# A software-pipelined windowed-attention stack: the rotary halves are exchanged by accumulating DMAs, dense matmul runs are issued in two halves, and a norm, a copy and the squares of a LayerNorm change place

## The chip, the cores and the metric

The kernel runs on one core of a Trainium2 chip. Its time is the device time of one execution in microseconds. Six engines appear in the profile: PE (TensorE; its weight loads are shown apart as PEld), DVE (VectorE), ACT (ScalarE), POOL (GpSimd), SP (SyncE, which here only issues DMAs) and the DMA engines. Each compute engine runs its own instruction stream; the streams meet in semaphores.

## What is computed

The program computes two blocks with conditioned LayerNorms. The middle of it, and most of its time, is a stack of six layers of windowed attention and a gated feed-forward network, on a batch of 4, 1024 tokens each, width 128:

```python
for i in range(DEPTH):                                   # DEPTH = 6
    x = attn_layer(shift_tokens(x), Wqkv[i], q_scale[i], k_scale[i], Wo[i]) + x
    x = ffn_layer(shift_tokens(x), ln_g[i], ln_b[i], W1[i], b1[i], W2[i], b2[i]) + x

def attn_layer(x, Wqkv, qs, ksc, Wo):                    # 16 heads of 64
    q, k, v = (sh(t) for t in jnp.split(x @ Wqkv, 3, -1))
    q, k = l2norm(q) * qs, l2norm(k) * ksc
    q = q * cos * scale + rotate_half(q) * sin * scale   # rotary embedding
    k = k * cos * inv + rotate_half(k) * sin * inv
    out = local_attention(q, k, v)                       # windows of 32, each sees itself and the one before
    return out.transpose(0, 2, 1, 3).reshape(b, n, INNER) @ Wo
```

`ffn_layer` is a LayerNorm, a matmul to twice 341 channels, `a * gelu(gate)` and a matmul back. Everything is float32. Ahead of the stack stand one attention over all tokens (`theta_attention`) and a LayerNorm; behind it stand a scan over tokens and a mixture of experts (`recurrence_and_mixture`).

## The kernel before

`local_layers` first normalizes x in eight chunks of 512 tokens (`LayerNorm`: mean on PE, `centred` on DVE, squares on ACT, variance on PE, a Newton square root on DVE, a spread on PE, `normed` on DVE, output on ACT; each waits for the one before). Then 96 units of work, 16 blocks of 256 tokens times 6 layers, go through a software pipeline. `pipelined(eng, step)` runs one hand-written order, `step(at)`, on each engine, once per unit: `at(k)` is the unit that entered k steps ago, so one step works on six units at once: projections of q and k of `at(1)` and `at(2)`, scores, softmax and weighted values of `at(3)`, output projection of `at(4)`, feed-forward of `at(5)` and `at(6)`. Six steps fill the pipeline, a hardware loop of 45 iterations runs two steps each (an even and an odd one, because many buffers are doubled), six steps drain it.

What an engine does next is set by the written order alone. A PSUM area is written again only when its last reader is done (`vacated(...)` waits on those semaphores). There are three pairs of PSUM banks (`pairs[0]` to `pairs[2]`) and two single ones.

On PE the dense runs are `scores(x)` (two mask matmuls, L957, then 64 float32 matmuls, which the trace counts as 128, L964) and `weighted(x)` (the same number, L1001), each with its own weight load, x being the half of the unit's tokens. Around them stand `project` (L920), `values` (L977), `norms` (L930), `hidden` (L1054), `out_projection` (L1021), `spread` (L947), `probs_across` (L986), `outputs_across` (L1011) and the LayerNorm of the feed-forward part (L1029 mean, L1036 variance, L1044 spread).

The rotary embedding works on four parts i of 128 x 1024 values (i = 0, 1 keys, 2, 3 queries). DVE multiplies the projection by the cosine table into `mcos` (`rotate_cos`, L1272) and by the sine table into `msin` (`rotate_sin`, L1281); SP copies `msin` with even and odd partitions exchanged into `swapped` by two DMAs (`halves_across`, L756); POOL adds `mcos` and `swapped` into `ks` or `qr` (`rotated`, L873):

```python
dst = (ks if i < 2 else qr[u.odd])[:, 4 * g:4 * g + 4, :].rearrange("p g t -> p (g t)")
nc.gpsimd.tensor_tensor(dst, mcos[i % 2][:, :], swapped[:, :], ALU.add).then_inc(rope_add, 1)
```

Then `scale_keys` (L1320) multiplies `ks` by its inverse norms into `kr`, and `scores` reads `kr` and `qr`. Of the softmax, DVE takes row maxima (`maxima`, L1330, and the tiny L1332, `ebias`), ACT the exponentials (L1172), PE transposes (L986), ACT copies (`probsT`). `outputs` (L1348) scales the attention result into `o`; `gated` (L1393) writes `act_out`.

Of the kernel before, what the change touches and what calls it, by code (L numbers as in the profile page):

```python
# [137 lines left out]
class LayerNorm:  # L138


# [17 lines left out]
    def tensor_mean(self, pe, n, src, wide):  # L158
        nc, c = self.nc, self.const

        pe.wait_ge(self.normed_ready, START + n)
        nc.tensor.matmul(wide, c["mean_w"][:, :], src, start=True, stop=True).then_inc(self.mean_ready, 1)  # L162
# [35 lines left out]
    def vector_normed(self, dve, n, wide, gain):  # L198
        nc = self.nc
        dve.wait_ge(self.spread_ready, START + n + 1)  # L200
        dve.wait_ge(self.out_ready, START + n)
# [439 lines left out]
def local_layers(nc, const, t):  # L641

    ctx = ExitStack()
    with ctx:
# [43 lines left out]
        ln = LayerNorm(nc, ctx, "loc_ln", const, sem, (sq[:, 0, 0:CH], sq[:, 0, CH:], sq[:, 1, 0:CH]))  # L688
# [5 lines left out]
        hs_ready, qk_ps, sq_ready, rot, rope_add = sem("hs_ready"), sem("qk_ps"), sem("sq_ready"), sem("rot"), sem("rope_add")  # L694
        swap_ready = [sem(f"swap_ready{i}") for i in range(4)]
# [18 lines left out]

        def pipelined(eng, step):
# [4 lines left out]
            for s in range(FILL):  # L720
                step(filling(s))
            with nc.Fori(FILL // 2, TOTAL // 2, engines=bass.OrderedEngineSet([eng.engine]), hint_back_edge=True) as i:
                for odd in range(2):
                    step(lambda k: Unit(2 * i + (odd - k), (odd - k) % 2))
            for s in range(TOTAL, TOTAL + FILL):
                step(filling(s))

        @block.sync
        def _(sp):
# [16 lines left out]

            def halves_across(i, u):

                if u is None:
                    return  # L750
                after(sp, rot, u.n, 8, 2 * i + 2)
                own_wait(sp, passed)
                after(sp, rope_add, u.n, 4, i)
                own_wait(sp, passed)
                for half in range(2):
                    sp.dma_start(swapped[1 - half:P:2, :], msin[half:P:2, :]).then_inc(swap_ready[i], 16)  # L756
# [24 lines left out]
            def step(at, refill=lambda name: None):  # L781
                halves_across(1, at(2))
                refill("wk")
                halves_across(2, at(2))
                even_windows(0, at(3))
                halves_across(3, at(2))
                refill("wq")
                halves_across(0, at(1))
# [52 lines left out]
        def _(pool):  # L841
# [20 lines left out]
            def rotated(i, u):  # L862
# [1227 lines left out]
```

## Time and profile before

| | |
|---|---|
| median of 3 runs (lowest, highest) | 4979.43 us (4970.4, 4989.21) |
| the profiled execution | 4985.01 us, span 4983.1 us |
| mean granted clock of TensorE | 0.950 |
| busy share: PE, DVE, ACT, POOL | 81%, 74%, 63%, 22% |
| mean share of the 16 DMA engines of its largest queue | 20.4% |

The times of the groups below are microseconds from the start of the span. A busy share is a mean over all stages; a wait in brackets stands in front of the instruction that waited, with what released it. "issue" is a wait that ended with nothing that the profile shows.

### The profile page before, as it was taken

The numbers are of one execution on the slowest core, as the hardware profiler recorded it, in microseconds if no ns is written. First come the engines' busy times: TensorE is split into PE (matmuls) and PEld (weight loads), VectorE is DVE, ScalarE is ACT, GpSimd is POOL, SyncE is SP. The second block draws the span as 40 slices with busy tenths as digits, with TensorE's granted clock in tenths as the row PEclk, the third lists the DMA queues.
The fourth block names the chain that finished last, engine by engine and source line by source line (L and its number), as shares of the span: only waits on it lengthen the run. The fifth ranks groups of instructions, "written<-read, shape, count | busy, mean of one in ns | idle before, by whom it ended". The sixth has DMA issues, their size and how long they took to land. (4 is left out here: it accounts for less than half of the span.)

```text
span 4983.1 us, 174228 instructions
## 1 busy us (share of the span) xinstructions
PE 4053.0 (81%) x68188; PEld 2876.0 (58%) x68188; DVE 3701.7 (74%) x6683; ACT 3147.4 (63%) x8447; POOL 1095.9 (22%) x856
## 2 busy tenths in 40 slices
PE   7947888888888888888888888888888888886578
PEld 4725566665666666665666656666666666654234
DVE  4837777777777877777777777787777777774765
ACT  4715766666666666766666667667766667663233
POOL 0002222222222222222222222222222222220112
PEclk9959999999999999999999999999999999997688
DMA  0012222222222222222222222222222222220000
GB/s 26 1 58 82 72 76 73 75 91 78 70 77 71 82 85 78 76 74 74 88 82 77 74 76 80 87 78 78 74 74 90 83 78 73 75 75 24 0 7 11
DMA packets 126167, 336.76 MB, mean 68 GB/s; under 512 B 32592, under 2 KB 33744, under 8 KB 125264
## 3 DMA queue, kind: packets, MB, share of 16 engines
q1 hardware_dynamic: 125520, 326.63, 20.4%
q8 instruction: 590, 9.67, 0.9%
q14 instruction: 57, 0.47, 0.0%
HBM read 22.41 MB, written 2.10 MB: 5 GB/s over the span
## 5 line engine op out<-in xcount | busy, mean ns | idle before, releaser
L1172 ACT ACTIVATE loc_probs<-loc_pair,loc_ebias,loc_rnorm 128x64 f32<-128x64 f32 x3072 | 1200.6, 433 | 10.9 <-DVE loc_ebias L1332 7.8
L873 POOL TENSOR_TENSOR loc_ks<-loc_mcos,loc_swapped 128x1024 f32<-128x1024 f32 x192 | 452.1, 2354 | 1776.6 <-DVE loc_kr L1320 1375.0
L920 PE MATMUL loc_pair<-loc_hs,loc_wqk 128*128 128x256 f32 x3072 | 751.4, 388 | 47.5 <-issue 43.1
L873 POOL TENSOR_TENSOR loc_qr<-loc_mcos,loc_swapped 128x1024 f32<-128x1024 f32 x192 | 452.2, 2355 | 1270.6 <-DMA loc_swapped<-loc_msin 1204.6
L1172 ACT ACTIVATION_READ_ACCUMULATOR loc_probs<-loc_pair,loc_ebias,loc_rnorm 128x1 f32 x3072 | 719.6, 234 | 0.0
L920 PEld LDWEIGHTS loc_pair<-loc_hs,loc_wqk 128*128 128x128 f32 x3072 | 568.0, 192 | 151.9 <-issue 64.4
L1330 DVE TENSOR_REDUCE loc_mx<-loc_pair 128x8 f32<-128x512 f32 x384 | 264.5, 689 | 410.1 <-PE loc_pair L964 402.9
L1272 DVE SCALAR_TENSOR_TENSOR loc_mcos<-loc_pair,loc_scal,loc_tab 128x1024 f32<-128x1024 f32 x384 | 490.5, 1277 | 86.7 <-ACT loc_sq L1154 65.3
L1154 ACT ACTIVATE loc_sq<-loc_pair 128x1024 f32<-128x1024 f32 x384 | 396.9, 1034 | 204.2 <-PE loc_pair L920 204.2
L1281 DVE SCALAR_TENSOR_TENSOR loc_msin<-loc_pair,loc_scal,loc_tab 128x1024 f32<-128x1024 f32 x384 | 489.6, 1275 | 9.1 <-DMA loc_swapped<-loc_msin 8.9
L964 PE MATMUL loc_pair<-loc_kr,loc_qr 64*32 64x64 f32 x24576 | 322.9, 226 | 122.0 <-issue 121.4
L1183 ACT ACTIVATE loc_vodd<-loc_pair 128x1024 f32<-128x1024 f32 x192 | 196.9, 1025 | 349.2 <-DMA loc_veven<-loc_vodd 210.5
L977 PE MATMUL loc_pair<-loc_wv,loc_hs 128*64 128x512 f32 x1536 | 408.3, 656 | 1.6 <-DVE loc_o L1348 1.4
L964 PEld LDWEIGHTS loc_pair<-loc_kr,loc_qr 64*32 64x32 f32 x24576 | 273.9, 106 | 221.6 <-issue 219.2
L1332 DVE SCALAR_TENSOR_TENSOR loc_ebias<-loc_mx,loc_rnorm 128x8 f32<-128x8 f32 x384 | 379.8, 989 | 13.2
L1001 PE MATMUL loc_pair<-loc_veven,loc_probsT 64*32 64x64 f32 x12288 | 307.7, 226 | 86.2 <-issue 83.9
L1197 ACT ACTIVATE loc_oT<-loc_pair 128x1024 f32<-128x1024 f32 x192 | 195.0, 1016 | 271.0 <-PE loc_pair L1011 271.0
L1190 ACT ACTIVATE loc_probsT<-loc_pair 128x1024 f32<-128x1024 f32 x192 | 195.8, 1020 | 268.8 <-PE loc_pair L986 268.8
L1021 PE MATMUL loc_one<-loc_oT,loc_wo 128*128 128x256 f32 x1536 | 347.5, 379 | 0.8 <-DVE loc_act_out L1393 0.4
L1001 PEld LDWEIGHTS loc_pair<-loc_veven,loc_probsT 64*32 64x32 f32 x12288 | 261.5, 105 | 149.6 <-issue 148.7
L1054 PE MATMUL loc_one<-loc_h,loc_w 128*128 128x256 f32 (+1 forms) x1152 | 322.1, 403 | 17.1 <-DVE loc_act_out L1393 7.3
L1001 PE MATMUL loc_pair<-loc_vodd,loc_probsT 64*32 64x64 f32 x12288 | 314.9, 226 | 3.7 <-issue 3.7
(228 smaller groups left out, 7457.6 us busy)
## 6 DMA issues: line engine op xcount, KB each, us to landing
loc_swapped<-loc_msin SPq DMA_DIRECT2D x768, 256.0 KB, 2.6
loc_veven<-loc_vodd SPq DMA_DIRECT2D x768, 64.0 KB, 2.2
loc_veven<-loc_vodd SPq DMA_DIRECT2D x384, 128.0 KB, 2.3
loc_wqk<-wqk_dram SPq DMA_DIRECT2D x12, 512.0 KB, 4.6
loc_wv<-wv_dram SPq DMA_DIRECT2D x6, 512.0 KB, 4.1
loc_wo<-wo_dram SPq DMA_DIRECT2D x6, 512.0 KB, 4.5
x<-xT_dram SPq DMA_DIRECT2D x1, 2048.0 KB, 7.4
loc_tab<-tables_dram SPq DMA_DIRECT2D x1, 2048.0 KB, 7.6
```

Source lines behind the costliest of these rows:

```text
L873: nc.gpsimd.tensor_tensor(dst, mcos[i % 2][:, :], swapped[:, :], ALU.add).then_inc(rope_add, 1)
L920: ins = nc.tensor.matmul(pairs[b][:, p // 2, (p % 2) * UNIT:(p % 2 + 1) * UNIT], wqk[:, k, w:w + P], hs[u.odd][:, :], start=True, stop=True)
L964: ins = nc.tensor.matmul(pairs[b][WIN * w:WIN * w + WIN, hp, p * 2 * WIN:(p + 1) * 2 * WIN], qr[u.odd][part, p, at:at + WIN], kr[u.odd][pa ...
L977: ins = nc.tensor.matmul(pairs[b][hp * DH:(hp + 1) * DH, g, :], hs[u.odd][:, BLK * x + DH * g:BLK * x + DH * g + DH], wv[:, hp, :], start= ...
L1001: ins = nc.tensor.matmul(pairs[b][WIN * w:WIN * w + WIN, hp, p * DH:(p + 1) * DH], probsT[part, p, WIN * w:WIN * w + WIN], v[part, w // 2, ...
L1021: ins = nc.tensor.matmul(bank(b)[:, 0:UNIT], wo[:, p, :], oT[:, p, :], start=p == 0, stop=p == PAIRS - 1)
L1054: ins = nc.tensor.matmul(bank(b)[0:FB[j], k * UNIT:(k + 1) * UNIT], w1[:, at:at + FB[j]], h[:, :], start=True, stop=True)
L1154: nc.scalar.activation(sq[:, i, :], flat(b), ACT.Square).then_inc(sq_ready, 1)
L1172: ins = nc.scalar.activation(probs[x][:, p, hp, :], pairs[b][:, hp, p * 2 * WIN:(p + 1) * 2 * WIN], ACT.Exp, bias=ebias[x][:, k:k + 1], sc ...
L1272: nc.vector.scalar_tensor_tensor(mcos[i % 2][:, :].rearrange("p (g t) -> p g t", g=4), flat(b).rearrange("p (g t) -> p g t", g=4), scal[u. ...
L1281: nc.vector.scalar_tensor_tensor(msin[:, :].rearrange("p (g t) -> p g t", g=4), flat(b).rearrange("p (g t) -> p g t", g=4), scal[u.odd][:, ...
L1332: nc.vector.scalar_tensor_tensor(ebias[x][:, k], mx[x][:, k], -1.0, rnorm[u.odd][:, x, HEADS:].rearrange("p (g y) -> p y g", y=2)[:, hp, : ...
```

## The change

1. Rotary: `rotate_cos` writes straight into `ks` or `qr` (`ks` is now doubled), `rotate_sin` writes into `msin[i % 2]`, and POOL issues two DMAs per part that add the exchanged halves into place. SP's copies, POOL's additions, `mcos`, `swapped` and the semaphore `rope_add` are gone; `landed` waits for the DMAs.
2. PE: in even steps `scores(1)`, `weighted(0)` and `scores(0)` are issued in two halves with other matmuls between, and the head of PE's loop is put at a fixed place, `head_slot` 208.
3. `ln_squares` moves from the start of ACT's step to DVE, behind `centre`.
4. On DVE `widen(0)` (the copy of the inverse norms, L1309) moves ahead of `rotate_cos(0)`.
5. The LayerNorm ahead of the stack takes chunks in pairs, with two sets of buffers, and the wait for the constants with two casts stands behind it.

```diff
-        mcos = [sb(f"mcos{i}", [P, HALF_Q]) for i in range(2)]
-        msin, swapped = sb("msin", [P, HALF_Q]), sb("swapped", [P, HALF_Q])
-        qr, ks = [sb(f"qr{i}", [P, PAIRS, UNIT]) for i in range(2)], sb("ks", [P, PAIRS, UNIT])
+        msin = [sb(f"msin{i}", [P, HALF_Q]) for i in range(2)]
+        qr, ks = ([sb(f"{s}{i}", [P, PAIRS, UNIT]) for i in range(2)] for s in ("qr", "ks"))
...
-                for half in range(2):
-                    sp.dma_start(swapped[1 - half:P:2, :], msin[half:P:2, :]).then_inc(swap_ready[i], 16)
...
+                after(pool, rot, u.n, 8, 2 * i + 2)
                 own_wait(pool, passed)
-                g = i % 2
-                dst = (ks if i < 2 else qr[u.odd])[:, 4 * g:4 * g + 4, :].rearrange("p g t -> p (g t)")
-                nc.gpsimd.tensor_tensor(dst, mcos[i % 2][:, :], swapped[:, :], ALU.add).then_inc(rope_add, 1)
+                for half in range(2):
+                    there = rotated_part(i, u)[1 - half:P:2, :, :].rearrange("p g t -> p (g t)")
+                    pool.dma_start(there, msin[i % 2][half:P:2, :], accum_op=ALU.add).then_inc(swap_ready[i], 16)
...
+            with nc.Fori(FILL // 2, TOTAL // 2, engines=bass.OrderedEngineSet([eng.engine]), hint_back_edge=True,
+                         head_slot={eng.engine: 208} if eng is nc.tensor else None) as i:
...
-                    scores(1, at(3), 2)
+                    scores(1, at(3), 2, whole if odd else (0,))
...
+                if not odd:
+                    scores(1, at(3), 2, (1,))
...
-                    weighted(0, at(3), 1)
+                    weighted(0, at(3), 1, whole if odd else (0,))
...
+                if not odd:
+                    weighted(0, at(3), 1, (1,))
                 if at(2) is not None:
                     vacated(pe, ((o_ready, at(3), 4, 2), (rot, at(1), 8, 2),))
-                    scores(0, at(2), 1)
+                    scores(0, at(2), 1, whole if odd else (0,))
...
+                if not odd:
+                    scores(0, at(2), 1, (1,))
                 ln_mean(at(4), 4)
...
-                after(dve, swap_ready[i - 1], u.n - (i == 0), SWAP, SWAP)
+                landed(dve, i - 2, u.n - (i < 2))
...
             def step(at, odd):
                 maxima(0, 1, at(3), 1)
                 centre(at(5), 4)
+                ln_squares(at(5))
...
+                widen(0, at(2))
                 rotate_cos(0, at(1), 1)
-                widen(0, at(2))
...
                 for c in range(2):
-                    ln.vector(dve, b * 2 + c, x[:, bass.ds(b * SEQ + c * CH, CH)], bank(0), bank(1)[:, 0:4], mods[:, 1:2])
+                    lns[c].vector_centre(dve, b * 2 + c, x[:, bass.ds(b * SEQ + c * CH, CH)], bank(c))
+                for c in range(2):
+                    lns[c].vector_rstd(dve, b * 2 + c, bank(2 + c)[:, 0:4])
+                for c in range(2):
+                    lns[c].vector_normed(dve, b * 2 + c, bank(c), mods[:, 1:2], b * 2)
```

The order of PE in the even step of the loop, around `scores(1)`, before (L957 mask, L964 scores, L920 `project(3)`, L977 `values(1)`, L930 `norms`; the counts are of instructions in the code, and the trace shows each float32 matmul as two, x128 for x64):

```order
L957 MATMUL loc_pair<-loc_mask,loc_ident 128x512 x2
L964 MATMUL loc_pair<-loc_kr,loc_qr 32x64 x64
L920 MATMUL loc_pair<-loc_hs,loc_wqk 128x256 x4
L977 MATMUL loc_pair<-loc_wv,loc_hs 64x512 x4
L134 ISA
L127 ISA
L930 MATMUL loc_one<-loc_sq,loc_head_sum 32x256 x16
```

The same place of the change (L961, L968, L919, L982 and L929 are the same calls):

```order
L961 MATMUL loc_pair<-loc_mask,loc_ident 128x512 x2
L968 MATMUL loc_pair<-loc_kr,loc_qr 32x64 x32
L919 MATMUL loc_pair<-loc_hs,loc_wqk 128x256 x4
L968 MATMUL loc_pair<-loc_kr,loc_qr 32x64 x32
L982 MATMUL loc_pair<-loc_wv,loc_hs 64x512 x4
L134 ISA
L127 ISA
L929 MATMUL loc_one<-loc_sq,loc_head_sum 32x256 x16
```

The second half of the scores now stands behind `project(3)`.

The end of PE's even step before, behind `weighted(0)` (L1054 `hidden(2)`, L986 `probs_across(1)`, L1011 `outputs_across(0)`, L947 `spread(1)`, L1029 `ln_mean`):

```order
L1001 MATMUL loc_pair<-loc_vodd,loc_probsT 32x64 x2
L134 REGISTER_ALU
L1054 MATMUL loc_one<-loc_h,loc_w 85x256 x2
L986 MATMUL loc_pair<-ident,loc_probs 128x128 x8
L957 ISA
L957 MATMUL loc_pair<-loc_mask,loc_ident 128x512 x2
L964 MATMUL loc_pair<-loc_kr,loc_qr 32x64 x64
L1011 MATMUL loc_pair<-ident,loc_o 128x128 x8
L134 REGISTER_ALU
L947 MATMUL loc_pair<-ident,loc_rk_wide 128x128 x8
L1029 MATMUL loc_one<-loc_xb,mean_w 128x256
```

The same place of the change, from the last row of `weighted(0)` (L1007) on; its first half stands ahead of `hidden(2)` (L1061):

```order
L1007 MATMUL loc_pair<-loc_vodd,loc_probsT 32x64 x2
L725 ISA
L961 ISA
L961 MATMUL loc_pair<-loc_mask,loc_ident 128x512 x2
L968 MATMUL loc_pair<-loc_kr,loc_qr 32x64 x32
L1018 MATMUL loc_pair<-ident,loc_o 128x128 x8
L134 REGISTER_ALU
L946 MATMUL loc_pair<-ident,loc_rk_wide 128x128 x8
L968 MATMUL loc_pair<-loc_kr,loc_qr 32x64 x32
L1036 MATMUL loc_one<-loc_xb,mean_w 128x256
```

Now nothing stands between the last matmul of `weighted(0)` and the mask of `scores(0)`, and the scores end behind `spread(1)`.

## Rows read from the trace of the kernel before

**Rows 1.** Busy time by stretch: the six filling steps, the loop

```profile
core 0: us, PE busy (x) PEld busy (x) DVE busy (x) ACT busy (x) POOL busy (x), PEclk, DMA share, GB/s
...
345.00:498.00 153.00, 115.08 (x2077) 83.60 (x2078) 106.08 (x160) 78.41 (x239) 42.13 (x30) 0.90 0.24 81
498.00:4417.00 3919.00, 3289.26 (x61935) 2394.85 (x61934) 3055.70 (x5315) 2689.48 (x7564) 956.20 (x721) 0.98 0.25 78
```

**Rows 2.** Who PE waited for, 500 to 4400: total us, times, longest

```profile
PE loc_one L930 <- DVE loc_act_out L1393: 134.0, 81, 2.3
PE loc_pair L964 <- issue: 117.9, 90, 2.2
PE loc_pair L1001 <- issue: 81.3, 88, 1.5
PE loc_pair L947 <- ACT loc_probs L1172: 76.4, 86, 0.9
PE loc_one L1036 <- ACT loc_lsq L1204: 61.5, 50, 1.4
PE loc_one L1044 <- DVE loc_rstd L95: 52.4, 41, 1.8
PE loc_one L1063 <- issue: 46.4, 44, 1.6
PE loc_pair L920 <- issue: 29.5, 43, 1.1
```

**Rows 3.** Timeline of PE, one even step: start, us, instruction, idle before

```profile
2273.07 1.94 PE L977 MATMUL loc_pair<-loc_wv,loc_hs 128*64 128x512 f32 x8
...
2291.22 0.25 PE L1001 MATMUL loc_pair<-loc_veven,loc_probsT 64*32 64x64 f32 x2 [1.23 <-issue]
...
2291.50 1.09 PE L1054 MATMUL loc_one<-loc_h,loc_w 128*85 128x256 f32 x4
2292.43 1.04 PE L986 MATMUL loc_pair<-ident,loc_probs 128*128 128x128 f32 x8
2293.30 0.59 PE L957 MATMUL loc_pair<-loc_mask,loc_ident 128*128 x2
2293.83 1.28 PE L964 MATMUL loc_pair<-loc_kr,loc_qr 64*32 64x64 f32 x95
2297.04 0.46 PE L964 MATMUL loc_pair<-loc_kr,loc_qr 64*32 64x64 f32 x33 [1.93 <-issue]
```

**Rows 4.** The page's DMA queues, the one that brings instructions: packets, MB, share

```profile
q8 instruction: 590, 9.67, 0.9%
```

**Rows 5.** The page's costliest groups: DVE's smallest operation

```profile
L1332 DVE SCALAR_TENSOR_TENSOR loc_ebias<-loc_mx,loc_rnorm 128x8 f32<-128x8 f32 x384 | 379.8, 989 | 13.2
```

**Rows 6.** Timeline of DVE, the same iteration

```profile
2256.18 1.91 DVE L1332 SCALAR_TENSOR_TENSOR loc_ebias<-loc_mx,loc_rnorm 128x8 f32<-128x8 f32 x1
...
2277.57 1.27 DVE L1281 SCALAR_TENSOR_TENSOR loc_msin<-loc_pair,loc_scal,loc_tab 128x1024 f32<-128x1024 f32 x1
...
2291.66 1.29 DVE L1348 TENSOR_TENSOR loc_o<-loc_pair,loc_recip 128x512 f32<-128x512 f32 x2 [0.70 <-PE loc_pair L1001]
...
2298.51 0.17 DVE L1332 SCALAR_TENSOR_TENSOR loc_ebias<-loc_mx,loc_rnorm 128x8 f32<-128x8 f32 x1
```

**Rows 7.** Timeline of POOL, the same iteration

```profile
2255.73 2.35 POOL L873 TENSOR_TENSOR loc_ks<-loc_mcos,loc_swapped 128x1024 f32<-128x1024 f32 x1 [14.18 <-DVE loc_kr L1320]
```

**Rows 8.** The page's DMA issues: KB each, median us from issue to landing

```profile
loc_swapped<-loc_msin SPq DMA_DIRECT2D x768, 256.0 KB, 2.6
```

**Rows 9.** Timeline of all engines ahead of the stack and in its LayerNorm

```profile
253.86 0.34 SPq L733 DMA_DIRECT2D loc_tab<-tables_dram  x1
...
262.67 0.43 DVE L1248 CAST loc_mask<-loc_sq 128x512 bf16<-128x512 f32 x1 [13.82 <-DMA loc_params<-params_dram]
...
283.34 2.07 PE L162 MATMUL loc_pair<-x,mean_w 128*128 x2 [0.93 <-DVE loc_sq L202]
...
293.32 2.07 PE L162 MATMUL loc_pair<-x,mean_w 128*128 x2 [0.93 <-DVE loc_sq L202]
```

More of the change, by code:

```diff
@@ L713, in local_layers, with rotated_part, landed @@
         LAST_USE = {"wk": 1, "wq": 1, "wv": 2, "wo": 3, "w1": 4, "w2": 5}
+        def rotated_part(i, u):
+            g = 4 * (i % 2)
+            return (ks if i < 2 else qr)[u.odd][:, g:g + 4, :]
+        def landed(eng, i, n):
+            if not isinstance(n, int) or n >= 0:
+                eng.wait_ge(swap_ready[i], SWAP * n + SWAP)
         def pipelined(eng, step):
@@ L720, in pipelined @@
             for s in range(FILL):
-                step(filling(s))
-            with nc.Fori(FILL // 2, TOTAL // 2, engines=bass.OrderedEngineSet([eng.engine]), hint_back_edge=True) as i:
+                step(filling(s), s % 2)
+            with nc.Fori(FILL // 2, TOTAL // 2, engines=bass.OrderedEngineSet([eng.engine]), hint_back_edge=True,
+                         head_slot={eng.engine: 208} if eng is nc.tensor else None) as i:
                 for odd in range(2):
-                    step(lambda k: Unit(2 * i + (odd - k), (odd - k) % 2))
+                    step(lambda k: Unit(2 * i + (odd - k), (odd - k) % 2), odd)
             for s in range(TOTAL, TOTAL + FILL):
-                step(filling(s))
+                step(filling(s), s % 2)
         @block.sync
@@ L1064, in ffn_out, with step @@
                 ins.then_inc(y_ps, 1)
-            def step(at):
+            whole = (0, 1)
+            def step(at, odd):
                 if at(2) is not None:
@@ L1197, in outputs_out @@
                 nc.scalar.activation(oT[:, :, BLK * x:BLK * x + BLK], flat(b).rearrange("p (g t) -> p g t", g=PAIRS), ACT.Copy).then_inc(oT_ready, 1)
-            def ln_squares(u):
-                if u is None:
-                    return
-                after(act, xc_ready, u.n)
-                after(act, var_ps, u.n - 1)
-                nc.scalar.activation(lsq[:, :], xc[:, :], ACT.Square).then_inc(lsq_ready, 1)
             def h_out(u):
@@ L1219, in gelus, with step @@
                                      bias=fpar[u.odd][0:FB[j], 3 + NFB + j:4 + NFB + j]).then_inc(gelu_ready, 1)
-            def step(at):
-                ln_squares(at(5))
+            def step(at, odd):
                 square(2, at(2), 2)
@@ L1315, in scale_keys @@
                 after(dve, spread_ps, u.n, 2, x + 1)
-                after(dve, rope_add, u.n, 4, 2)
+                for i in range(2):
+                    landed(dve, i, u.n)
                 after(dve, sim_ps, u.n - 2, 2, 2)
@@ L1405, in residual_ffn, with step @@
                 ins.then_inc(xa_done, 1)
-            def step(at):
+            def step(at, odd):
                 maxima(0, 1, at(3), 1)
                 centre(at(5), 4)
+                ln_squares(at(5))
                 gated(2, at(6), 3)
```

127 lines of the change are left out of this document (67 added, 60 removed).

## The prediction

> **What bounds the kernel now.** I read the stretches first [rows 1]: the loop runs from 498 to 4417, 45 iterations in 3919 us, so 87.1 us for two steps, and the six filling steps take 153 us, the draining ones about as long. PE is busy for 3289.26 / 45 = 73.1 us of an iteration, DVE for 67.9, ACT for 59.8; the granted clock is 0.98, so TensorE stands at its upper level all through the loop and the clock has nothing to give. No engine is full. What ends an iteration is PE's chain, and it is idle for 14.0 of 87.1 us. The second view is whom PE waited for [rows 2]; divided by the 3900 / 87.1 = 44.8 iterations of its window, the idle time is
>
> - issue (nothing that the profile shows): (117.9 + 81.3 + 46.4 + 29.5) / 44.8 = 6.1 us
> - `act_out` from DVE ahead of `norms`: 3.0 us
> - `probs` from ACT ahead of `spread`: 1.7 us
> - `lsq` from ACT: 1.4 us; `rstd` from DVE: 1.2 us
>
> That is 13.4 of the 14.0 us. The change goes at each of these but the third.
>
> What the issue waits are: in the timeline of PE [rows 3] one ends at 2291.22 inside `weighted(0)` and the next at 2297.04 inside `scores(0)`. Between them stand 16 matmuls (eight rows of two, of which the first is shown) + 4 + 8 + 2 + 95 = 125, each with a weight load, 250 instructions and a few register and semaphore instructions. The queue that brings instructions moved 9.67 MB in 590 packets, 16.4 KB each [rows 4]. Both fit one reading: PE's code comes in blocks of about 256 instructions, and a block that is used up faster than the next one arrives leaves PE waiting. A dense run (128 matmuls with 128 loads) uses a whole block in some 1.5 us (1.28 us for 95 of 128 matmuls [rows 3]), every other piece of the step takes several times that for as many instructions. In the even half dense runs and block ends meet, in the odd half they don't; the counts in [rows 2], 43 to 90, are one or two for an iteration.
>
> What makes DVE late: `ebias`, 128 x 8 values, takes 0.17 us alone and 1.91 us at 2256.18, where it ends with POOL's addition of 2255.73 + 2.35 = 2258.08 [rows 6, 7]. Its mean over 384 is 0.989 us [rows 5], 0.82 us too much; there are 384 / 96 = 4 in a step and 8 in an iteration, so this smallest operation alone loses 6.6 us of DVE's 67.9: DVE stands still while POOL adds. The small steps of the two Newton roots stand in the same place.
>
> The Trainium skill (SBUF — State Buffer, section Who interferes with whom) says that a DVE instruction with two SBUF inputs contends with a GpSimd instruction that reads SBUF, and that the later one is fully blocked. By that, the trace agrees: `ebias` reads two SBUF tiles, and 1.91 against 0.17 us is the block. The same page has a rule that speaks against this change: a DMA of GpSimd's queue needs descriptors that GpSimd writes itself, and VectorE's copies in two-port modes starve it. No row here shows it; its price is taken up under the third rival.
>
> **The change part by part.** Per iteration of the loop, against 87.1 us.
>
> *Rotary.* Removed: POOL's eight additions of 2.35 us and SP's sixteen issues. DVE's own multiplications stay as they are (1.27 us [rows 6]), with another destination. Added: sixteen DMA issues on POOL. POOL is busy for 956.20 / 45 = 21.2 us of 87.1 [rows 1], of which 8 x 2.35 = 18.8 us goes away, so even at 4 us an issue it has room. DVE is no longer blocked. I credit only what PE waits for: of the 3.0 us ahead of `norms` the half that the blocks make (see below for the other half), **-1.6 us**; of `rstd` all, -1.2 us. From below this part could give nothing, if DVE is blocked by the issues as it is by the additions; from above 4.2.
>
> What must land in time: queries of part 3. `rotate_sin(3)` ends at 2277.57 + 1.27 = 2278.84 [rows 6], and the mask of `scores(0)` starts at 2293.30 [rows 3], 14.5 us later. Today an exchange takes 2.6 us from issue to landing [rows 8], the addition 2.35 more. No row shows a DMA that adds, so its cost lies between those 2.6 us and anything; I take twice a plain one for each of the pair, some 10 us together, and it is hidden by `norms` to `probs_across(1)`. The keys have longer still. The work behind it on POOL, the copy of the next tokens, waits for two issues more; `project(0)` needs it, but two halves later.
>
> *Splits and the loop's place.* The order shows PE's even step cut after 32 of 64 matmuls, with 1.9 to 2 us of `project(3)` behind the first half, and so on. Kept are the issue waits ahead of the split runs: at `project(2)` 29.5 / 43 = 0.7, at the first `weighted(1)` 0.6 (the mean of its 88 waits is 0.92, the second of each pair 1.23 [rows 2, 3]) and in the feed-forward's last matmuls 46.4 / 44 = 1.05: 2.3 us. Gone or shrunk: 1.2 in `weighted(0)` and 117.9 / 44.8 = 2.6 in the two `scores`, 3.8 us; I leave 0.3 us of them: **-3.5 us**. From below: if half a run is still too dense, half of it, -1.9.
>
> The splits also add waits. The second half of `weighted(0)` now stands straight ahead of the mask of `scores(0)`, which waits for `outputs(0)`, the reader of that pair, two operations in 1.29 us [rows 6]. Before, `hidden(2)` and `probs_across(1)` stood between, 2293.30 - 2291.50 = 1.8 us [rows 3]. With the hops of the semaphores **+1.3 us**. And `scores(1)` ends 2 us later, while DVE's row maxima, `ebias`, the residual and `gated(0)` still stand ahead of `act_out`: about 3.7 us of work, with only `values(1)`, 1.94 us [rows 3], to cover it. So of `norms`' wait, 1.4 us stays in the even half; that is the other half of the 3.0 above.
>
> *Squares to DVE, the copy ahead.* DVE squares 256 columns in about 0.4 us and PE need not wait for ACT's queue: **-1.4 us** (`lsq`), and with `rstd` above **-2.5 us** in all. DVE has room: 67.9 less at least 6.6 of blocks. `widen(0)` first: ahead of `spread(0)`, which waits for ACT's `probs` and not for the copy, so nothing.
>
> *Handed on.* The wait on ACT's `probs`, 0.9 us in each half, stays: ACT's row of two times eight exponentials and a table load is no shorter. Once PE is early at `outputs_across(1)` in the odd half, it meets the `probs` of `exponentials(0, 1)` there. Between 0 and all of the 2.5 us saved ahead of it; ACT is only 59.8 / 81 busy, so it is latency, not load, and I take **+0.5 us**.
>
> *LayerNorm ahead.* A chunk takes 293.32 - 283.34 = 10.0 us [rows 9], nearly all of it one engine waiting for another. In a pair the second chunk runs in the gaps of the first; I take 15 us a pair, so -5 us times four pairs, -20 (bounds 0 and -40). It also begins without the constants: DVE stood for 13.8 us until 262.67, SP began to load at 253.86 [rows 9]: another -8. **-28 us** in all.
>
> **Sum.** -1.6 - 2.5 - 3.5 + 1.3 + 0.5 = -5.8 us an iteration, 81.3 instead of 87.1, times 45 = -261 us. Filling and draining have the same waits in emptier steps (PE busy 115 of 153 us while filling): -15. With -28: -304. Against the profiled execution, 4985.01, this gives 4681; it lay 5.6 us above the median, so 4675 us.
>
> **The rivals.**
>
> *First, the same mechanisms with other sizes.* If the halves of runs still wait for code, or ACT takes back all that DVE gives (+2 instead of +0.5), an iteration saves 3 us: 135 + 15 + 28, so about 4800. If both new waits are covered and the code waits at the head fall too, it saves 8: about 4580. For the first speaks that four things must hold at once; for the second, that the next limit is PE's own 73.1 us.
>
> *Second, the additions land late (the other side, slower).* Each microsecond by which part 3 lands after the mask of `scores(0)` is ready costs a microsecond in each of the 96 steps. The gain is 304 / 96 = 3.2 us a step, so the change loses when from the end of `rotate_sin(3)` to landing more than 14.5 + 3.2 = 17.7 us pass. At 20 us it is 5.5 x 96 - 304 = +224: 5200 us. For it speaks that two DMAs of 256 KB that read, add and write are issued by POOL, behind other issues, by a way that no row shows; against it that 17.7 us is nearly seven times the 2.6 us of a plain one [rows 8], and that the DMA engines are busy for 25% [rows 1].
>
> *Third, DVE is blocked all the same.* POOL's descriptor work may hold DVE as its additions do, or DVE's copies may hold POOL. Then the 1.6 and 1.2 us are not saved, the late scores add 1.4 us ahead of `norms`, and the square, now in front of the root, is blocked too, as are operations that sixteen issues meet where eight additions did not; for these I take 1.6 us, two blocks as in [rows 6]. -3.5 - 1.4 + 1.3 + 0.5 + 1.4 + 1.6 = -0.1 us an iteration; with the LayerNorm's -28 it is about 4945, no change that can be told from none with certainty.
>
> By the skill's starvation rule, named above, `widen`'s float32 copies would hold up POOL's issues where DVE and POOL meet; what that does to the time is the second rival's price, and no row shows such a meeting.
>
> **How the numbers follow.** Main case, 4590 to 4750: 0.60. Smaller gain, 4750 to 4870: 0.17. Larger gain, 4500 to 4590: 0.08. DVE still blocked, 4920 to 5000: 0.05. Late landing, over 5005: 0.10. The predicted time is the main one's, 4675. From 4560 to 4850 lies 0.8 of it: the main case, most of the smaller gain and a part of the larger. Runs of before spread by 0.4%, so about 0.5% is what a measurement can tell from no change: below 4954 is faster, 0.86; same 0.04; slower 0.10.
>
> **What would show it.** Right: `ebias` at 0.17 us throughout and DVE's busy time in the loop down by 6 us an iteration or more; no waits for `lsq` and `rstd`; issue waits of about 2.5 us an iteration, none in the `scores` and the second `weighted`; a new wait for `o` of over 1 us ahead of the mask; `act_out` at 1.4 us in even halves alone; an iteration of 80 to 83 us. Wrong: a wait of PE for the accumulating DMAs ahead of L961, `ebias` still near 1 us, issue waits that only moved to the other halves, or a wait on ACT's `probs` of over 3 us an iteration.

## The result and the profile after

The changed kernel takes 4730.99 us (median of 4 runs, 4725.08 to 4750.15), the kernel before 4978.07 us: a ratio of 0.9509, interval 0.9476 to 0.9541. 247 us were saved; 304 had been forecast (4675 us), and 4731 us lies inside the range of 4560 to 4850. The profiled execution has a span of 4723.2 us, 259.9 less than before.

First the stretches of the changed kernel; the columns are those of [rows 1]. They are the LayerNorm ahead of the stack, the filling steps, the loop, the draining steps and the tail.

```profile
249.00:303.00 54.00, 33.86 (x113) 19.97 (x114) 27.85 (x118) 16.52 (x24) 1.85 (x9) 0.61 0.25 95
303.00:450.00 147.00, 117.34 (x2085) 84.82 (x2084) 91.78 (x164) 79.91 (x239) 36.30 (x50) 0.91 0.44 86
450.00:4161.00 3711.00, 3287.78 (x61924) 2385.57 (x61925) 2541.97 (x5402) 2658.90 (x7471) 741.14 (x1080) 0.98 0.41 82
4161.00:4308.00 147.00, 116.68 (x2040) 83.85 (x2039) 75.61 (x194) 86.03 (x251) 12.84 (x20) 0.92 0.23 47
4308.00:4723.30 415.30, 282.42 (x865) 141.39 (x864) 261.84 (x571) 120.58 (x165) 74.62 (x75) 0.76 0.02 8
```

Against [rows 1] the loop is 3711 us long instead of 3919, so an iteration is 82.5 us instead of 87.1: 208 us. It begins at 450 instead of 498. Of these 48 us the filling steps give 6 (147 instead of 153) and the LayerNorm with its start 42. The remaining 4 us lie behind the loop. PE's busy time in the loop is what it was (3287.78 against 3289.26 us), so all the gain of the loop is idle time of PE. DVE's busy time has fallen from 67.9 to 56.5 us an iteration.

Whom PE waits for in the changed kernel, 480 to 4200, 45.1 iterations (compare [rows 2]; L961 is the mask, L929 `norms`, L946 `spread`, L1007 `weighted`, L982 `values`, L919 `project`, L1061 `hidden`, L1043 the variance):

```profile
PE loc_pair L961 <- DVE loc_o L1363: 116.8, 90, 2.0
PE loc_one L929 <- DVE loc_act_out L1415: 96.2, 50, 2.2
PE loc_pair L946 <- ACT loc_probs L1187: 61.8, 71, 0.9
PE loc_pair L1007 <- issue: 53.2, 47, 1.6
PE loc_pair L982 <- issue: 18.5, 44, 0.8
PE loc_pair L919 <- issue: 16.5, 38, 2.8
PE loc_one L1061 <- DVE loc_act_out L1415: 16.2, 46, 0.4
PE loc_one L1043 <- DVE loc_lsq L1391: 11.1, 44, 0.3
PE loc_pair L1007 <- DVE loc_kr L1335: 10.2, 45, 0.2
...
PE loc_one L929 <- issue: 7.3, 25, 0.3
```

An iteration has 2.1 us of issue waits (6.1 before) and none of note in the scores. `rstd` is gone from the list and `lsq` is 0.25 us (2.5 before for both). But `o` has risen from 0.2 to 2.6 us, and `act_out` is still 2.1 us ahead of `norms`, where 1.4 had been forecast, and 0.4 us more ahead of `hidden`.

The even step of the changed kernel in PE's timeline, 2290 to 2315, shows what the splits brought:

```profile
2292.98 1.93 PE L929 MATMUL loc_one<-loc_sq,loc_head_sum 128*32 128x256 f32 x32 [2.17 <-DVE loc_act_out L1415]
...
2306.24 1.10 PE L1061 MATMUL loc_one<-loc_h,loc_w 128*85 128x256 f32 x4 [0.35 <-DVE loc_act_out L1415]
2307.37 1.09 PE L991 MATMUL loc_pair<-ident,loc_probs 128*128 128x128 f32 x8
...
2311.19 0.60 PE L961 MATMUL loc_pair<-loc_mask,loc_ident 128*128 x2 [1.94 <-DVE loc_o L1363]
2311.72 1.11 PE L968 MATMUL loc_pair<-loc_kr,loc_qr 64*32 64x64 f32 x64
2312.76 1.97 PE L1018 MATMUL loc_pair<-ident,loc_o 128*128 128x128 f32 x8
```

The mask stands behind the second half of `weighted(0)` and waits 1.94 us for `outputs(0)`. What follows is slower as well: `outputs_across` lasts 1.97 us, against 1.09 us for the eight matmuls of the same shape in `probs_across` (L991). The granted clock of the stretches around the waits, with the columns of [rows 1], shows why:

```profile
2293.00:2297.00 4.00, 4.00 (x43) 2.85 (x44) 2.93 (x7) 2.39 (x5) 1.19 (x2) 1.00 0.34 81
...
2300.00:2306.00 6.00, 4.97 (x87) 3.94 (x85) 3.68 (x6) 5.97 (x20) 1.92 (x3) 1.00 0.60 149
...
2311.00:2315.00 4.00, 3.81 (x77) 3.23 (x78) 2.56 (x3) 0.23 (x1) 1.46 (x2) 0.60 0.04 7
2315.00:2320.00 5.00, 4.77 (x154) 3.94 (x155) 3.03 (x6) 4.25 (x13) 0.73 (x2) 0.98 0.54 102
```

The granted clock is 1.00 ahead of the wait of 1.94 us and 0.60 for the 4 us behind it, mostly the lower of its two levels (1.2 of 2.4 GHz), then 0.98. By these rows this wait costs up to 4 x 0.4 = 1.6 us more (an estimate). Not every wait does: behind the 2.17 us ahead of `norms`, 18 us earlier, the clock stays at 1.00 (first row). What tells the two apart is not shown by any run here.

In DVE's timeline, the same place:

```profile
2309.29 1.29 DVE L1363 TENSOR_TENSOR loc_o<-loc_pair,loc_recip 128x512 f32<-128x512 f32 x2 [1.97 <-PE loc_pair L1007]
...
2317.62 0.17 DVE L1347 SCALAR_TENSOR_TENSOR loc_ebias<-loc_mx,loc_rnorm 128x8 f32<-128x8 f32 x1
```

`ebias` takes 0.17 us again. Below are its group in the changed kernel and, from its page, the cost and landing of the accumulating DMAs:

```profile
L1347 DVE SCALAR_TENSOR_TENSOR loc_ebias<-loc_mx,loc_rnorm 128x8 f32<-128x8 f32 x384 | 85.7, 223 | 13.2
...
L868 POOL DMA_DIRECT2D loc_qr<-loc_msin x384 | 332.1, 1006 | 1150.8 <-DVE loc_msin L1295 1133.1
...
loc_ks<-loc_msin POOLq DMA_DIRECT2D x384, 256.0 KB, 4.4
loc_qr<-loc_msin POOLq DMA_DIRECT2D x384, 256.0 KB, 5.0
```

The mean of `ebias` is 223 ns, not 168, its median: POOL still has one small addition that reads SBUF, on the keys (`loc_kr`, L878, 0.60 us). One of them starts at 2319.53, and the `ebias` of 2319.78 takes 0.39 us.

An issue holds POOL for 1.0 us, the landing comes 5.0 us after it (median; 7.7 at the longest): some 6 to 7 us for a pair, where I had taken 10, and far inside the 14.5 us of room.

The LayerNorm ahead of the stack, PE's mean matmuls of two successive pairs of chunks:

```profile
262.75 3.78 PE L163 MATMUL loc_pair<-x,mean_w 128*128 x4 [0.93 <-DVE loc_sq L203]
...
274.83 3.78 PE L163 MATMUL loc_pair<-x,mean_w 128*128 x4 [0.93 <-DVE loc_sq L203]
```

12.1 us a pair, where one chunk took 10.0 [rows 9].

### The profile page after: what moved, and what is told of

Read it like the earlier page. It is cut to its first block and busy times, and to the rows that moved or that the text cites. A ratio compares the mean times of both kernels' runs of the same rounds, so it can differ in the third digit from the quotient of the medians.

```text
span 4723.2 us, 172910 instructions
## 1 busy us (share of the span) xinstructions
PE 4045.2 (86%) x68188; PEld 2863.9 (61%) x68188; DVE 3161.6 (67%) x6779; ACT 3116.9 (66%) x8351; POOL 867.3 (18%) x1240
## 2 busy tenths in 40 slices
DMA packets 126144, 336.58 MB, mean 71 GB/s; under 512 B 32592, under 2 KB 33744, under 8 KB 125264
## 5 line engine op out<-in xcount | busy, mean ns | idle before, releaser
L919 PE MATMUL loc_pair<-loc_hs,loc_wqk 128*128 128x256 f32 x3072 | 745.8, 386 | 25.5 <-issue 17.3
L1187 ACT ACTIVATION_READ_ACCUMULATOR loc_probs<-loc_pair,loc_ebias,loc_rnorm 128x1 f32 x3072 | 709.7, 231 | 0.0
L919 PEld LDWEIGHTS loc_pair<-loc_hs,loc_wqk 128*128 128x128 f32 x3072 | 568.8, 191 | 122.0 <-issue 40.5
L868 POOL DMA_DIRECT2D loc_ks<-loc_msin x384 | 331.5, 1008 | 1278.7 <-DVE loc_msin L1295 1242.0
L868 POOL DMA_DIRECT2D loc_qr<-loc_msin x384 | 332.1, 1006 | 1150.8 <-DVE loc_msin L1295 1133.1
L982 PE MATMUL loc_pair<-loc_wv,loc_hs 128*64 128x512 f32 x1536 | 373.2, 606 | 21.7 <-issue 19.3
L1363 DVE TENSOR_TENSOR loc_o<-loc_pair,loc_recip 128x512 f32<-128x512 f32 x384 | 246.5, 683 | 212.3 <-PE loc_pair L1007 212.1
L1061 PE MATMUL loc_one<-loc_h,loc_w 128*128 128x256 f32 (+1 forms) x1152 | 338.6, 419 | 25.6 <-DVE loc_act_out L1415 24.1
L1007 PE MATMUL loc_pair<-loc_vodd,loc_probsT 64*32 64x64 f32 x12288 | 304.2, 226 | 55.2 <-issue 55.1
L968 PEld LDWEIGHTS loc_pair<-loc_kr,loc_qr 64*32 64x32 f32 x24576 | 268.7, 106 | 111.8 <-issue 111.7
L968 PE MATMUL loc_pair<-loc_kr,loc_qr 64*32 64x64 f32 x24576 | 317.1, 228 | 4.3 <-issue 4.2
L1028 PEld LDWEIGHTS loc_one<-loc_oT,loc_wo 128*128 128x128 f32 x1536 | 291.6, 190 | 41.4 <-DVE loc_act_out L1415 1.2
L1007 PE MATMUL loc_pair<-loc_veven,loc_probsT 64*32 64x64 f32 x12288 | 299.9, 226 | 12.8 <-DVE loc_kr L1335 11.2
L1286 DVE SCALAR_TENSOR_TENSOR loc_ks<-loc_pair,loc_scal,loc_tab 128x1024 f32<-128x1024 f32 x192 | 245.8, 1280 | 85.6 <-ACT loc_sq L1169 84.6
```

The lines of the kernel that those rows point to most:

```text
L868: pool.dma_start(there, msin[i % 2][half:P:2, :], accum_op=ALU.add).then_inc(swap_ready[i], 16)
L919: ins = nc.tensor.matmul(pairs[b][:, p // 2, (p % 2) * UNIT:(p % 2 + 1) * UNIT], wqk[:, k, w:w + P], hs[u.odd][:, :], start=True, stop=True)
L968: ins = nc.tensor.matmul(pairs[b][WIN * w:WIN * w + WIN, hp, p * 2 * WIN:(p + 1) * 2 * WIN], qr[u.odd][part, p, at:at + WIN], kr[u.odd][pa ...
L982: ins = nc.tensor.matmul(pairs[b][hp * DH:(hp + 1) * DH, g, :], hs[u.odd][:, BLK * x + DH * g:BLK * x + DH * g + DH], wv[:, hp, :], start= ...
L1007: ins = nc.tensor.matmul(pairs[b][WIN * w:WIN * w + WIN, hp, p * DH:(p + 1) * DH], probsT[part, p, WIN * w:WIN * w + WIN], v[part, w // 2, ...
L1028: ins = nc.tensor.matmul(bank(b)[:, 0:UNIT], wo[:, p, :], oT[:, p, :], start=p == 0, stop=p == PAIRS - 1)
```

## The experiments

The runs were made in three batches (e1 to e4, e5 to e8, e9 to e12; the last on another chip than the first two). Each has the ratio to the kernel before in its own batch, where that took 4980, 5001 and 4985 us, so ratios are compared, not times. The changed kernel itself was not run again beside the later batches; differences from its 0.9509 of some 0.5% are therefore not told from none.

**The splits undone, and the place undone.** The first run makes the three dense runs whole in even steps, with the loop head at its place:

```diff
-                    scores(1, at(3), 2, whole if odd else (0,))
+                    scores(1, at(3), 2)
...
-                if not odd:
-                    scores(1, at(3), 2, (1,))
```

and so for `weighted(0)` and `scores(0)`.

> The changed kernel with scores(1), weighted(0) and scores(0) whole again in even steps; PE's loop stays at its fixed place. Theory (the splits trade instruction waits for data waits): an iteration of the loop regains about 3.8 us of issue waits inside the scores and the second weighted, and loses the waits that the splits brought, o ahead of the mask (1.9 down to 0.3) and act_out ahead of norms (2.1 down to 0.5), so it is 82.5 + 0.6 = about 83.1 us, the kernel about 4760 us. Rival (the splits alone are what pays): data waits stay, an iteration is 86 us and the kernel about 4890 us.

4700.09 us, ratio 0.946 (0.9434 to 0.9486): not the 4760 us of the theory but, if anything, half a per cent faster than with the splits (the intervals just overlap). The traces' spans are 4698.1 and 4723.2 us, iterations 82.1 and 82.5 us. Whom PE waits for in it, 500 to 4100, 43.9 iterations (L968 scores, L1018 `outputs_across`):

```profile
PE loc_pair L1007 <- issue: 136.4, 89, 3.6
PE loc_pair L968 <- issue: 106.7, 86, 2.7
PE loc_pair L946 <- ACT loc_probs L1181: 79.7, 88, 1.0
PE loc_pair L1018 <- ACT loc_probs L1181: 32.2, 41, 0.9
PE loc_pair L961 <- DVE loc_o L1357: 28.8, 44, 0.7
```

The issue waits are back, 6.7 us an iteration instead of 2.1, and `o` is down to 0.65 and `act_out` to 0.2. The exchange itself is there: 4.6 us of code waits against 4.3 us of waits for DVE. The theory had the first term at 3.8, and it left out PE's own time: in the stretch 500 to 4000 PE is busy for 71.7 us an iteration (3057.80 of 3500) with whole runs and for 73.1 (3101.70 of 3500) with the splits, at a granted clock of 0.99 and 0.98. The splits' waits are followed by slower work more often, and that takes back what they win.

The second run takes away the place alone:

```diff
-            with nc.Fori(FILL // 2, TOTAL // 2, engines=bass.OrderedEngineSet([eng.engine]), hint_back_edge=True,
-                         head_slot={eng.engine: 208} if eng is nc.tensor else None) as i:
+            with nc.Fori(FILL // 2, TOTAL // 2, engines=bass.OrderedEngineSet([eng.engine]), hint_back_edge=True) as i:
```

> The changed kernel without the fixed place of PE's loop head; all else stays. Theory (instruction blocks of 256; where their ends fall decides): the loop's issue waits differ from 2.1 us an iteration, by up to 2 us either way, and they move to other lines. Rival (the splits alone make the waits small, the place means nothing): the same time within 10 us, 4731 us, with waits at the same lines.

4957.97 us, ratio 0.9968 (0.9951 to 0.9984). Without this one number nearly the whole change is lost: 227 us by the medians. I had expected up to 2 us an iteration; it was 5.2, and one line has most of it (L918 is `project(2)`, the first of an iteration; window 500 to 4100, 41 iterations):

```profile
PE loc_pair L918 <- issue: 192.6, 41, 5.2
PE loc_pair L960 <- DVE loc_o L1362: 106.3, 82, 2.0
```

4.7 us, once an iteration, at the loop's head. Its timeline there, the last matmul of one iteration, the first of the next, and the same `project(2)` run in the following step:

```profile
2285.51 0.86 PE L1035 MATMUL loc_one<-loc_xb,mean_w 128*128 128x256 f32 x2
2290.94 3.40 PE L918 MATMUL loc_pair<-loc_hs,loc_wqk 128*128 128x256 f32 x8 [4.57 <-issue]
...
2337.18 1.89 PE L918 MATMUL loc_pair<-loc_hs,loc_wqk 128*128 128x256 f32 x8
```

Behind the wait of 4.57 us the same eight matmuls take 3.40 instead of 1.89 us: the granted clock is 0.58 from 2290.9 to 2295 (1.00 until 2286), and 0.95 over this loop against 0.98.

**Why the place matters.** The page's row of the instruction queue has the number. First the changed kernel, then the one without the place:

```profile
q8 instruction: 591, 9.68, 0.9%
```

```profile
q8 instruction: 633, 10.37, 0.9%
```

42 packets more for 45 iterations: nearly one more an iteration. The loop has 2854 traced instructions of PE an iteration (2846 before). Between issue waits lie 256, and the first lies at the 48th with place 208, so 208 + 2854 = 3062 end within twelve blocks of 256 (3072). Without the place the waits lie some 13 instructions earlier, so the head is at about 221, and 221 + 2854 = 3075 reaches into a thirteenth. The kernel before, 2846 instructions long, has 590 packets [rows 4]: it did not spill. To test it I put the head 16 instructions later, and 32 earlier:

```diff
-                         head_slot={eng.engine: 208} if eng is nc.tensor else None) as i:
+                         head_slot={eng.engine: 224} if eng is nc.tensor else None) as i:
```

> The changed kernel with the loop head 16 instructions later, at place 224. Theory (the loop's 2854 traced instructions on TensorE fit twelve blocks of 256 from place 208, 208 + 2854 = 3062 of 3072; from 224 they spill into a thirteenth, 3078, which is fetched just as the loop jumps back): an issue wait of 4 to 5 us at the first project of each iteration, 45 x 4.7 = 210 us more, the kernel about 4950 us. Rival (the distance of dense runs to block ends is what counts, and 16 instructions shift it little): 4731 us within 30 us.

> The changed kernel with the loop head 32 instructions earlier, at place 176; it fits twelve blocks too. Theory (only the spill matters much): the same time, 4731 us within 40 us, with the issue waits at other instructions. Rival (208 is a sharp best place): over 4800 us.

Place 224: 4988.39 us, ratio 0.9978 (0.9958 to 0.9997), 633 packets, an iteration of 88.7 us, and the wait at the head:

```profile
PE loc_pair L919 <- issue: 180.8, 40, 4.9
```

4.5 us an iteration, as foretold. Place 176: 4801.22 us, ratio 0.960 (0.9565 to 0.9635), 590 packets, 84.3 us an iteration and no such wait. So the spill is worth 0.9978 - 0.960 = 3.8% between two places of one batch, and 0.9978 - 0.9509 = 4.7% against place 208. The exact place among those that fit makes 0.960 - 0.9509 = 0.9%, about 45 us: a little more than the theory's margin of 40, and short of the rival's 4800 us once the batch's slower kernel before is allowed for. With place 176 the issue waits are (64.6 + 39.8 + 11.5) / 41.5 = 2.8 us instead of 2.1, and PE is busy for 74.2 us an iteration instead of 73.1.

**The rotary part alone**, on the kernel before, with the head left to itself and at place 208. The edit is parts 2 to 5 of the change taken back, in the second with the place of part 2 kept.

> The kernel before with the rotary part of the change alone (accumulating DMAs from GpSimd, no additions on it). Theory (GpSimd's additions block VectorE, which is late at act_out and rstd): ebias falls from a mean of 0.99 to 0.17 us, VectorE's busy time by 10 us an iteration, an iteration from 87.1 to about 83.5 us, the kernel about 4810 us. Rival (the exchange only leaves the path of SyncE, or nothing of it is on the path): 4950 to 4980 us.

> The kernel before with the rotary part alone, and PE's loop head at place 208. Theory (without the place this edit lost at the loop head what it gained elsewhere): the wait of 4.3 us at the first project goes, an iteration is 86.8 - 4 = about 82.8 us and the kernel about 4770 us. Rival (the wait at the head is the rotary part's own, for instance from the queue of DMAs): about 4940 us as without the place.

4941.98 us, ratio 0.9928 (0.9897 to 0.9959), and 4802.96 us, ratio 0.9613 (0.9582 to 0.9645). The first time is nearly the rival's (4950 to 4980 us), that nothing of the part is on the path, and yet the theory's marks are there: `ebias` has a mean of 223 ns instead of 989 [rows 5], and `rstd` is no wait any more. What hides the gain is the head of the loop, from PE's waits without the place (L911 is `project`) and from the page:

```profile
PE loc_pair L911 <- issue: 175.5, 41, 4.9
```

```profile
q8 instruction: 633, 10.37, 0.9%
```

With the place the wait is gone, and an iteration is 83.0 us instead of 86.8 (82.8 expected). The rotary part is the largest of the change, 3.9%; its few additional waits lengthen PE's loop by 8 instructions, and these lost it most of that until the head was moved. The kernel before with the place alone was not run. But it did not spill, and with the rotary part at place 208 the issue waits are 7.3 us an iteration, more than its 6.1, so the 3.9% do not come from the place. The wait for the squares stays, 1.1 us an iteration over 42.2 iterations:

```profile
PE loc_one L1036 <- ACT loc_lsq L1206: 46.0, 40, 1.4
```

**The LayerNorm part alone**, on the kernel before.

> The kernel before with the paired LayerNorm and the later wait for the constants alone. Theory: it saves what stood ahead of the loop in the two traces, 48 us less some 5 for the filling, so 4978 - 43 = about 4935 us, with pairs of chunks at 12.5 us each. Rival (my forecast's 15 us a pair): 4950 us.

4934.18 us, ratio 0.9918 (0.9887 to 0.9949): 46 us by the medians, 25 to 56 by the interval, in line with the 42 us of the two traces.

**What POOL's additions did to DVE.** Both runs give POOL work for nothing behind the accumulating DMAs of a part:

```diff
+                for k in range(3):
+                    after(pool, scr, u.n, 12, 3 * i + k)
+                    own_wait(pool, passed)
+                    nc.gpsimd.tensor_tensor(scratch[:, :], tab[:, 0, 0:320], tab[:, 1, 0:320], ALU.add).then_inc(scr, 1)
```

and the other with `nc.gpsimd.memset(scratch[:, :], 1.0)` in place of the addition.

> The changed kernel with work for nothing on GpSimd: behind each part's two DMAs three additions of 128 x 320 values read from two SBUF tables into a scratch tile, 24 in an iteration, some 0.75 us each. Nothing waits for them but GpSimd's own queue. Theory (GpSimd's additions block VectorE): ebias and the Newton steps are stretched again, VectorE's busy time rises by 5 to 10 us an iteration, and the kernel slows to about 4850 us. Rival (the blocks never were on the path, what the rotary part gained came from fewer waits between engines): under 4760 us.

> As the run before, with three fills of 128 x 320 values in place of the additions: GpSimd writes SBUF and reads nothing. Theory (it is GpSimd's reading that blocks): VectorE's busy time as without them, the same time, 4731 us within 20 us. Rival (any work of GpSimd on SBUF blocks VectorE): slower, as with the additions.

Additions: 4823.01 us, ratio 0.9682 (0.9663 to 0.9702); fills: 4762.89 us, ratio 0.9542 (0.9522 to 0.9563). The stretch 500 to 4000, with the columns of [rows 1], with the additions and then with the fills:

```profile
500.00:4000.00 3500.00, 3076.86 (x57255) 2226.06 (x57256) 2583.92 (x4987) 2451.65 (x6891) 1552.65 (x1996) 0.97 0.40 81
```

```profile
500.00:4000.00 3500.00, 3081.63 (x57478) 2231.12 (x57472) 2364.03 (x5025) 2469.86 (x6946) 1058.53 (x2005) 0.97 0.40 81
```

And the group of `ebias` in both, as in [rows 5], in the same order:

```profile
L1353 DVE SCALAR_TENSOR_TENSOR loc_ebias<-loc_mx,loc_rnorm 128x8 f32<-128x8 f32 x384 | 182.3, 475 | 13.1
```

```profile
L1353 DVE SCALAR_TENSOR_TENSOR loc_ebias<-loc_mx,loc_rnorm 128x8 f32<-128x8 f32 x384 | 86.4, 225 | 13.1
```

Per iteration DVE is busy for 2583.92 / 3500 x 84.2 = 62.2 us with additions and 2364.03 / 3500 x 83.8 = 56.6 with fills, the same as the changed kernel. So reading by POOL stretches DVE's operations, and writing alone does not. The fills are shorter (0.58 us each against 1.07 for an addition), but half the work would still show in DVE's busy time if it were the work as such, and nothing shows. The two differ by 1.4% in time on one chip, though DVE is not the engine that is full. By the rule of the Trainium skill, SBUF — State Buffer, section Who interferes with whom, that only a GpSimd instruction that reads contends with a two-input operation of DVE, this is what must come, and the traces agree. The fills' 4762.89 us is 12 us above the range that was expected for them; whether they cost 0.3% against the changed kernel stays open, since the intervals overlap (up to 0.9541 and from 0.9522).

**The squares back on ScalarE**, in the changed kernel:

```diff
             def step(at, odd):
+                ln_squares(at(5))
                 square(2, at(2), 2)
```

> The changed kernel with the squares of the feed-forward's LayerNorm on ScalarE again, first in its step. Theory (that wait was 1.4 us an iteration before, and PE then comes early to the next limit): the wait for lsq is 1.0 to 1.4 us an iteration instead of 0.25, an iteration is 0.5 to 1.2 us longer, the kernel 4755 to 4785 us. Rival (with VectorE no longer blocked, centre is early and ScalarE's squares are in time): no change, 4731 us within 15 us.

4763.29 us, ratio 0.9548 (0.9529 to 0.9568). The time is in the theory's range, but the run does not decide: it is 0.4% above the changed kernel's 0.9509 of another batch, with intervals that overlap, and the fills had 0.9542 in the same batch. The wait for `lsq` is

```profile
PE loc_one L1043 <- ACT loc_lsq L1219: 24.3, 39, 0.6
```

over 41.9 iterations, 0.6 us instead of 0.25: half of what the theory said. DVE's blocks are not what took the rest of the 1.4 us: with the rotary part alone it is still 1.1 us at place 208, and 1.3 without the place (55.3 us in the 41.5 iterations from 500 to 4100). On whole runs the squares' move shows more. From the rotary part with the place to the changed kernel with whole runs, which adds parts 3 to 5, an iteration goes from 83.0 to 82.1 us and the wait for `lsq` from 1.1 us to nothing. Moving `widen(0)` (part 4) has no run of its own.

**Against the waits of the splits.** Two runs put `gated(0)`, whose input has long been ready, ahead of DVE's work on the late scores; the first also moves `hidden(2)` behind the second half of `weighted(0)`, the second leaves `hidden(2)` and puts the second half ahead of `probs_across(1)`, which concerns even steps only. The diff of the second:

```diff
+                gated(0, at(5), 4)
                 maxima(1, 0, at(3), 2)
                 residual_ffn(at(6), 3)
                 maxima(1, 1, at(3), 2)
-                gated(0, at(5), 4)
...
-                if at(3) is not None:
-                    vacated(pe, ((kr_ready, at(2), 2, 1),))
-                    probs_across(1, at(3), 2)
                 if not odd:
                     weighted(0, at(3), 1, (1,))
+                if at(3) is not None:
+                    vacated(pe, ((kr_ready, at(2), 2, 1),))
+                    probs_across(1, at(3), 2)
```

> The changed kernel with two moves against the waits that the splits brought: gated(0) on VectorE ahead of maxima(1, 0), and on TensorE hidden(2) behind the second half of weighted(0). Theory (act_out is late only because VectorE handles the late scores first; the mask of scores(0) needs cover for outputs(0)): act_out ahead of norms from 2.1 us to under 0.5, o ahead of the mask from 1.9 to about 1.0 us, an iteration from 82.5 to about 80 us, the kernel about 4620 us. Rival (ScalarE's chain of exponentials is right behind and takes it back): the wait on probs grows by as much, 4710 to 4731 us.

> The changed kernel with gated(0) ahead of maxima(1, 0) on VectorE as in the run that had both moves, but hidden(2) stays between the halves of weighted(0) in even steps, and probs_across(1) stands behind the second half. Theory (probs_across covers the wait for o, and hidden covers that for the keys): the 2.2 us an iteration of waits for kr ahead of probs_across go, o is 1.6 us in both halves together, an iteration is about 79.3 us and the kernel at 0.913 of before, about 4545 us. Rival (ScalarE's chain takes it back): the wait on probs grows, 0.925 as with both moves.

4627.95 us, ratio 0.9255 (0.9223 to 0.9287), and 4610.93 us, ratio 0.9237 (0.9211 to 0.9263): both clearly faster than the changed kernel, by 2.7 and 2.9%, and not to be told from each other. Iterations are 80.6 and 79.9 us. In the first the wait for `o` is 0.9 us an iteration and that for `act_out` is gone, as expected, but PE now waits 2.3 us for `kr` ahead of `probs_across`. Whom PE waits for in the second, 500 to 4000, 43.8 iterations:

```profile
PE loc_pair L1007 <- issue: 87.4, 113, 2.9
PE loc_pair L961 <- DVE loc_o L1363: 68.8, 86, 1.1
PE loc_pair L946 <- ACT loc_probs L1187: 51.6, 70, 0.9
PE loc_pair L919 <- DVE loc_msin L1295: 33.5, 44, 1.2
```

`act_out` has left the head of the list (0.3 us), `o` is 1.6 us, the wait for `kr` ahead of `probs_across` is gone, and ACT's `probs` did not grow (1.2 us). So the part of the rival that says why falls; its 0.925 for the time, no gain over the first, is what was measured within the interval. Against the expected 79.3 us an iteration 0.6 is missing, which is about half of what separates 0.9237 from the expected 0.913. Two waits that grew from the first run to the second make these 0.6: 0.3 us for `act_out` ahead of `hidden`, and issue, 3.0 us in all instead of 2.7, now in `weighted` 2.6 times an iteration. DVE's `rotate_sin` is late by 0.8 us at a projection in both. The granted clock in this loop is 1.00. I did not run these two moves with whole runs.

## Why the prediction was right, and where its steps were off

**What bounds the kernel** held: PE's chain with its idle time, and five causes of it. The saving of the loop is 4.6 us an iteration, forecast 5.8. One reading was wrong: that at a mean granted clock of 0.98 the clock has nothing to give. With whole runs PE's busy time is 1.4 us an iteration lower, and a mean of 0.98 holds stretches at 0.60.

**Rotary, -1.6 and -1.2 us.** The mechanism is shown, by `ebias`, by DVE's busy time (-11.4 us an iteration, "6 or more" had been said) and by the two runs with POOL's work put back. Alone and with the loop head in place it saves 3.9%, 87.1 to 83.0 us an iteration: the wait for `act_out` falls from 3.0 to 0.2 us and that for `rstd` to nothing. That is the 1.6 and 1.2 us and the other 1.4 of the 3.0, which the prediction set aside because the splits would keep them. It did not take the 1.4 us of `lsq`; they were rightly given to the move of the squares, which with the rotary part in place had 1.1 us left to win.

**Splits and place, -3.5 and +1.3 us and the 1.4 that stays.** As a sum this step failed: it made the splits worth 0.8 us an iteration, and by the two traces they cost 0.4. These 1.2 us, 54 us in the kernel, are nearly all that the loop saved less than forecast. Its terms are not far off one by one: the issue waits fell by 4.6 us against whole runs, the wait for `o` rose by 1.9 (+1.3 forecast), that for `act_out` ahead of `norms` from 0.2 to 2.1, in even halves (1.4 forecast). Mis-sized are the last two; `outputs(0)` begins only when the second half's last matmul is done, and the hops on both sides make 1.94 us of an operation pair of 1.29. What was missing is PE's own time: 73.1 us an iteration with the splits, 71.7 with whole runs, for the same work. The slower clock behind some of the waits is the likely cause; its rows are above, but no run changed the clock alone.

**The place** I took for part of the splits, and it was the step that I understood least. The waits "ahead of the split runs" are as forecast (2.1 us of issue in all, 2.3 + 0.3 said). But that the other parts lengthen PE's loop by 8 instructions, that the code then ends in a thirteenth block, and that this costs 4.7 us an iteration is nowhere in the prediction. It came out right because 208 avoids it.

**Handed on, +0.5 us.** `probs` fell to 1.4 us instead of rising to 2.2. In the kernel with whole runs it is 2.6 us (79.7 and 32.2 over 43.9 iterations), near the forecast; the splits' waits on DVE seem to hide ACT's lateness here.

**LayerNorm, -28 us.** It was 42 to 46: 12.1 us a pair, not 15, and its first matmul starts at 250.1 instead of 263.7, not 8 us earlier. Filling and draining gave -6 each (147 instead of 153 us), -12 where -15 had been said. So the 14 to 18 us too little here hide a part of what the splits lack, and that is luck.

**Rivals.** Late landing is refuted for this kernel, with 6 to 7 us of the 14.5. DVE blocked by POOL's issues is refuted: DVE is busy for 56.5 us an iteration, the median of `ebias` is 168 ns, and the longest of 384 takes 449. `widen`'s copies do not hold up the issues either: 92 of the 768 issues ran beside such a copy, and none of these took over 0.88 us, while others took up to 1.22. The smaller gain, 4750 to 4870, begins 19 us above the measured time.

## What to carry to other kernels

Look at the instruction queue's packets per iteration when a loop on TensorE is long (2854 instructions here): if an edit of a few instructions elsewhere costs some us once an iteration at the first matmul, the body has grown into one more block, and moving the loop head gives it back. An edit that seems worth nothing should be measured again with the head in its old place, since it may hide a gain of 4%. A dense run that is cut moves its end, and the end is what others wait for; here the cuts alone won nothing, and paid only with further moves. Put something between the second half and the next work on the same PSUM pair, and move an engine's work with old inputs ahead of that on the late ones. A small operation of VectorE that takes ten times its shortest duration (1.91 against 0.17 us) was here the sign that GpSimd was reading SBUF.

## What was not expected of the hardware

- Reaching into a thirteenth block of 256 instructions costs 4.5 to 4.7 us an iteration at the head of the loop, though in the wait of 4.57 us only one packet of the instruction queue is under way, for 1.2 us. Why the wait is that long is not settled.
- Some waits of PE are paid twice: behind one of 1.94 us the granted clock was 0.60 for 4 us, behind one of 4.57 us eight matmuls took 3.40 instead of 1.89 us, while behind one of 2.17 us the clock stayed at 1.00; and the mean granted clock of the loop was 0.95 with that wait, 0.98 in the changed kernel and 1.00 with the two moves.
- An accumulating DMA of 64 partitions by 4 KB from GpSimd holds it for 1.0 us and lands after 4.4 to 5.0 us (medians); a plain one from SyncE landed after 2.6 [rows 8]. With about the same bytes moved in all (336.58 MB, 336.76 before) the DMA engines' mean busy share in the loop rose from 0.25 to 0.41.
